# FFN weight split in two halves, and the context sum and small columns moved from VectorE to GpSimd, in a fused attention block on one Trainium2 core

## The reference

```
xn = layernorm(x)                        # no gain, no bias
# branch 1: linear attention and a gated feed-forward net (FFN)
q, k, v = split(xn @ Wqkv + bqkv);  qp, kp = elu(q) + 1, elu(k) + 1
attn = (qp @ (kp.T @ v)) / (qp @ sum(kp) + 1e-6)
x1 = layernorm(xn + attn) * g1 + b1
s = layernorm(x1 + (silu(x1 @ Wg + bg) * (x1 @ Wu + bu)) @ Wd + bd) * g2 + b2
# branch 2: three cycles that couple blocks of the features
gf = global_net(mean(xn over positions))          # 3 small layers, one value per batch
out = xn
repeat 3 times:
    tf = coupling_net(out)                        # 4 layers, one value per position
    out = out + (0.1 + range * (0.7*gf + 0.3*tf - 0.5) * 2) * twist(out)
result = x + s * silu(out)
```

## Time and profile before

| | |
|---|---|
| median of three runs | 165.39 us (165.28 to 165.51) |
| profiled execution, its own time | 163.89 us |
| its span in the trace | 162.1 us |
| PE busy, share of the span | 152.6 us, 94% |
| DVE busy | 137.4 us, 85% |
| ACT busy | 131.6 us, 81% |
| POOL busy | 116.9 us, 72% |
| mean granted PE clock | 0.986 of full |

### The profile page before, as it was taken

The page is one execution under the profiler, slowest core; times in us unless marked ns, Lnnn a source line. Parts: engine busy times, 40 slices in busy tenths (PEclk is TensorE's granted clock), DMA queues, the critical chain, the costliest instruction groups (busy, mean ns, idle before and its releaser), DMA issues.

```text
span 162.1 us, 3409 instructions
## 1 busy us (share of the span) xinstructions
PE 152.6 (94%) x934; PEld 117.0 (72%) x934; DVE 137.4 (85%) x549; ACT 131.6 (81%) x345; POOL 116.9 (72%) x202
## 2 busy tenths in 40 slices
PE   7889999999999899999999999999999999999940
PEld 7567988888888595545554565788888888888840
DVE  2998699899988998299999968978767999978893
ACT  3989796998999978999999986995648985844950
POOL 0078676699981869995089597379999998896573
PEclk9999999999999999999999999999999999999995
DMA  5997333030230000000000000000000110110113
GB/s 172 256 382 167 65 67 69 0 69 19 50 65 0 2 6 0 0 0 4 0 0 0 4 4 0 0 0 4 0 0 7 60 65 6 65 67 0 65 65 129
DMA packets 11923, 7.83 MB, mean 48 GB/s; under 512 B 8961, under 2 KB 9729, under 8 KB 11905
## 3 DMA queue, kind: packets, MB, share of 16 engines
q1 hardware_dynamic: 11472, 7.28, 15.5%
q10 hardware_dynamic: 432, 0.34, 0.6%
HBM read 3.43 MB, written 2.10 MB: 34 GB/s over the span
## 4 chain that ended last, share of the span: by engine, by line
PE 82%; ACT 7%; issue 3%; DMA 2%; DVE 2%; POOL 2%; POOLq 0%; ACTq 0%; DVEq 0%
PE bank L1074 11%; PE bank L1266 10%; PE bank L1191 7%; PE bank L1255 7%; PE bank L1257 7%; PE bank L1256 7%; PE bank L1203 4%; PE bank L1145 4%; PE bank L1216 4%; PE bank L1132 3%; PE bank L1133 3%; PE bank L1136 3%; PE bank L1156 3%; DMA col<-in_cols 2%; PE bank L1281 2%
## 5 line engine op out<-in xcount | busy, mean ns | idle before, releaser
L515 ACT ACTIVATE pq<-bank,bffn 128x512 f32<-128x512 f32 (+1 forms) x24 | 16.1, 682 | 9.3 <-PE bank L1257 9.3
L271 POOL TENSOR_TENSOR rstd<-ve,minus_half 128x4 f32<-128x4 f32 x21 | 21.2, 1011 | 1.7
L816 DVE SCALAR_TENSOR_TENSOR pq<-bank,bffn,pq 128x512 f32<-128x512 f32 (+1 forms) x24 | 17.6, 739 | 5.2 <-issue 2.4
L1255 PE MATMUL bank<-x_hi,ffn_hi 128*128 128x512 f32 (+1 forms) x48 | 20.5, 427 | 0.0
L1256 PE MATMUL bank<-x_lo,ffn_hi 128*128 128x512 f32 (+1 forms) x48 | 18.9, 395 | 0.0
L1257 PE MATMUL bank<-x_hi,ffn_lo 128*128 128x512 f32 (+1 forms) x48 | 18.9, 394 | 0.0
L1266 PEld LDWEIGHTS bank<-wd,pq 128*128 128x128 f32 x144 | 17.9, 191 | 1.3
L1266 PE MATMUL bank<-wd,pq 128*128 128x128 f32 x144 | 18.0, 274 | 0.0
L455 ACT ACTIVATE q_stage<-bank,col 128x512 f32<-128x512 f32 x24 | 16.0, 677 | 0.1
L269 POOL TENSOR_SCALAR nm<-mv 128x4 f32<-128x4 f32 x21 | 4.7, 223 | 15.4 <-DVE mv L653 15.4
L323 POOL TENSOR_TENSOR ab<-cpl 128x8 f32<-128x8 f32 x4 | 9.7, 2426 | 8.1 <-ACT cpl L487 8.0
(11 more groups left out here) (174 smaller groups left out, 457.7 us busy)
## 6 DMA issues: line engine op xcount, KB each, us to landing
x_tok<-in_x SPq DMA_DIRECT2D x8, 256.0 KB, 6.8
tx_tok<-xn_tok SPq DMA_DIRECT2D x16, 128.0 KB, 2.4
out<-pq SPq DMA_DIRECT2D x6, 256.0 KB, 2.0
r_tok<-in_w_ffn SPq DMA_DIRECT2D x1, 341.0 KB, 6.8
r_tok<-in_w_first SPq DMA_DIRECT2D x1, 320.0 KB, 3.5
out<-pq SPq DMA_DIRECT2D x2, 128.0 KB, 1.7
out<-pq ACTq DMA_DIRECT2D x1, 256.0 KB, 2.2
row<-in_rows SPq DMA_DIRECT2D x1, 192.0 KB, 6.3
```

Of the source, the lines that this page charges most:

```text
L271: return pool.tensor_tensor(rstd[i][:, b], ve[i][:, b], minus_half[:], ALU.pow)
L816: dve.scalar_tensor_tensor(out=hid[b % 2][0:m, c], in0=up_of(n)[0:m], scalar=bffn[0:m, CHUNKS + c:CHUNKS + c + 1], in1=sg[n % 2][0:m], op0 ...
L1255: pe.matmul(dst[0:m], ffn_hi[:, w], x1_hi[:, b], start=True, stop=False)
```

## The change

Four edits. ACT's split of the FFN weights becomes two instructions of 341 columns: the first behind tile 3 of batch 0, as the whole one was, the second behind tile 2 of batch 1. DVE's `ffn_lo` becomes two instructions too, behind `feature_k(6)` and at the end of batch 1's pass. `small_columns` goes from DVE to the head of POOL's pass 7 (`bias_rows`, once called in it, stays on DVE at its place). `ctx_sum` goes from DVE to the end of POOL's pass 7, as two instructions with a link between them, since POOL adds the offset and the two sums in separate steps.

```diff
+FFN_AFTER = ((0, 3), (1, 2))
...
+            def join_sums():
+
+                pool.wait_ge(sums_ready, 1)
+                pool.wait_ge(xT_hi_ready, BATCHES - 1)
+                pool.wait_ge(xT_lo_ready, BATCHES)
+                link(pool.tensor_scalar(ctx_sum[:], sum_hi, -OFFSET * SEQ, 0.0, ALU.add, ALU.add))
+                pool.tensor_tensor(ctx_sum[:], ctx_sum[:], sum_lo, ALU.add).then_inc(ctx_ready, 1)
+
+            def small_columns():
+
+                pool.wait_ge(cols_loaded, 16)
+                pool.tensor_scalar(half_b4[:], col[:, COL["cn_b4"]:COL["cn_b4"] + 1], 0.5, 0.0, ALU.mult, ALU.add)
...
             for b in range(BATCHES + 2):
                 if b + 2 < BATCHES:
                     norm_x(b + 2)
+                if b == BATCHES - 1:
+                    small_columns()
                 if b >= 2:
                     rstd_of(1, b - 2)
...
                 for done in {6: (0, 1, 2), 7: (3, 4, 5), 8: (6,), 9: (7,)}.get(b, ()):
                     negate_twisted(done)
+                if b == BATCHES - 1:
+                    join_sums()
...
+            def split_ffn(k):
+
+                act.wait_ge(ffn_loaded, 16)
+                act.wait_ge(cols_loaded, 16)
+                act.mul(ffn_hi[:, k * HID:(k + 1) * HID], ffn_raw[:, k * HID:(k + 1) * HID],
+                        col[:, COL["g1"]:COL["g1"] + 1]).then_inc(ffn_hi_ready, 1)
...
+                    if (b, t) in FFN_AFTER:
+                        split_ffn(FFN_AFTER.index((b, t)))
...
+            def ffn_low(k):
+
+                ks = slice(k * HID, (k + 1) * HID)
+                dve.wait_ge(ffn_hi_ready, k + 1)
+                dve.scalar_tensor_tensor(out=ffn_lo[:, ks], in0=ffn_raw[:, ks], scalar=col[:, COL["g1"]:COL["g1"] + 1],
+                                         in1=ffn_hi[:, ks].bitcast(F32), op0=ALU.mult,
+                                         op1=ALU.subtract).then_inc(ffn_ready, 1)
...
-                if b == BATCHES - 1:
-                    dve.wait_ge(sums_ready, 1)
-                    dve.wait_ge(xT_lo_ready, BATCHES)
-                    dve.scalar_tensor_tensor(out=ctx_sum[:], in0=sum_hi, scalar=-OFFSET * SEQ, in1=sum_lo,
-                                             op0=ALU.add, op1=ALU.add).then_inc(ctx_ready, 1)
...
                 feature_k(TILES * b + 1)
                 if b == 0:
-                    small_columns()
+                    bias_rows()
...
                 feature_k(TILES * b + 2)
+                if b == 1:
+                    ffn_low(0)
...
-            pe.wait_ge(ffn_ready, 1)
+            pe.wait_ge(ffn_ready, 2)
```

More of the change, by code:

```diff
@@ L293, in add_rows_to @@
                 return pool.tensor_tensor(yb[b % 2][:, ts], yb[b % 2][:, ts], x_tok[:, b, ts], ALU.add)
+            def join_sums():
[7 more added lines that the diff above has]
+                pool.tensor_scalar(half_b4[:], col[:, COL["cn_b4"]:COL["cn_b4"] + 1], 0.5, 0.0, ALU.mult, ALU.add)
+                pool.tensor_scalar(half_gb3[:], col[:, COL["gc_b3"]:COL["gc_b3"] + 1], 0.5, 0.0, ALU.mult, ALU.add)
+                pool.tensor_scalar(gain[:, 0:1], col[:, COL["range"]:COL["range"] + 1], W_GLOBAL, 0.0, ALU.mult, ALU.add)
+                pool.tensor_scalar(gain[:, 1:2], col[:, COL["range"]:COL["range"] + 1], W_TOKEN, 0.0,
+                                   ALU.mult, ALU.add).then_inc(cols_ready, 1)
             def norm_x1(b):
@@ L997, in _ @@
                 if b == 1:
[L998 to L1001, removed]
+                    ffn_low(1)
             add_eps(BATCHES - 2)
```

## The result

The changed kernel takes 171.31 us (median of four runs, 171.11 to 171.76) against 165.33 for the kernel before beside it: a ratio of 1.0363, with a 95% interval of 1.0341 to 1.0386. The prediction was +6.5 us and 171.9. The profiled execution took 171.11 us with a span of 169.3 us, 7.2 us more than the 162.1 of before; the medians differ by 6.0 us. The two numbers are not in conflict. Over all sessions the kernel before had medians of 165.33, 164.82, 164.65 and 164.42 us. Where time and span of an execution are both on record, the time was 1.8 to 3.1 us longer than the span, while the spans had medians of 162.1 to 162.3 us (23 executions in each of the three later sessions, 161.8 to 163.7).

A forecast was written before the change was run, and what follows sets the result against it. PE was taken to bound the kernel, busy for 152.6 of 162.1 us. A wait of 5.1 and a slow clock of 1.4 made +6.5 us on 165.39, so 171.9 us; range 170.2 to 173.5.

The forecast's parts named there:

- (b): Context sum behind POOL's pass 7: PE's matmul on it starts at 63.8 in place of 58.73, +5.1 us.
- faster: Rival: POOL's context sum comes in time for PE at 58.3 to 58.7; -0.6 us at most, 164.8 us; chance 0.02.
- (c): PE's clock falls while PE waits for the sum, then half pace for 3.2 us behind the wait: +1.4 us.
- a longer slow stretch: Rival: PE runs at half pace for 6.4 us behind the wait; +8.1 us, 173.5 us; chance 0.17.
- the first rival: PE waits for the sum, but its clock does not fall or is back at once: +5.1, 170.5 us; chance 0.16.
- the wait without the clock: Rival: only PE's wait for the sum is paid, no slow clock: +5.1, 170.5 us; chance 0.16.
- (a): Context sum leaves DVE: k-v copy starts 0.91 us earlier, PE's 0.6 us idle time goes; counted as nothing here.
- (d): Small columns leave DVE, four of 0.14 us at 12.45: they give nothing, 0.6 us at most without cover.
- (e): FFN split in halves on ACT and DVE in the early batches: 0, and 0.3 us at most either way.

The follow-up runs named there:

- the shorter waits: The changed kernel with POOL's sum earlier in pass 7, behind scale_x1 (first) or behind norm_x1 (second): 170.29 us and 168.82 us.

## Why the prediction was right

By its own steps:

(b), the wait, was forecast at +5.1 us with the matmul at 63.8. It started at 63.64, +4.9. Pass 7 began at 56.93 in place of 57.2, as POOL was free at 55.99 rather than 56.16 and the four small columns took 0.94 us rather than 1.04; the rest followed the rows: from its start to the sum's end 6.56 us, forecast 6.5. The chain that ended last lies on POOL for 8% of the span in place of 2%, some 10 us more, as foreseen. The sum moved alone gives all of the loss, and the sum at the head of the pass gives none of it. The rival "faster" had named its deciding point (the sum ready by 58.7), and at that point the loss did vanish. Its price of up to 0.6 us was too high: 0.27 us reached layer 2, and in that run other work took it back. That only 0.27 of 0.6 came through fits ACT, whose work on tiles 30 and 31 had no break there; this was read from the trace, not tested.

(c), the clock, was the mis-sized term: +1.4 us forecast, 2.3 measured, shown by the run that kept PE at work. I took the slow stretch from the start of the kernel, 3.2 us; here PE worked for 6.0 us at a granted 0.50. The forecast treated the length of the slow stretch as the same everywhere. The traces show 3.4, 5.2, 6.0 and 6.0 us of it in kernels that differ in little else. The second size was off as well, the other way: half of 6.0 us less 0.2 would be 2.8 us, and 2.3 were lost. The Trainium skill (TensorE: Matmul & The Clock Gate, Part 1) calls the number of slow products at a kernel's start run-variable, for one and the same kernel. The runs here show the stretch behind a wait, not that start, and it too differs between executions of one kernel (above, under the shorter waits).

So the length of the stretch was near that of the rival "a longer slow stretch" (6.4 us), not that of the forecast, and its cost lies between the forecast's 1.4 and the rival's 3.0. The time alone would hardly have told: 171.31 us lies 0.8 over the first rival's 170.5 and 0.6 under the forecast. It is the trace and the run with PE kept at work that rule out the wait without the clock.

Against the spans the two errors, -0.2 and +0.9, leave the forecast 0.7 us short (6.5 against 7.2). Against the medians it is 0.5 us too high (6.5 against 6.0). That it came so near there is in part luck: the carry assumed that the profiled execution stands to its median before as it does after. Before it was 1.5 us under its median, after it is 0.2 us under, and that difference of some 1.2 us turned 0.7 us too few into 0.5 us too many.

(a) was right in itself: DVE's copy started at 54.03 and PE did not wait for it, worth nothing here. (d) and (e) were right: 0, confirmed by the run with only these edits. In the changed kernel's ACT and DVE timelines the second half of the split sits at its new place, and ACT still idles before its next PE product:

```profile
18.40 0.61 ACT L451 ACTIVATE ffn_hi<-r_tok,col 128x341 fp32r<-128x341 f32 x1
18.89 0.38 ACT L441 ACTIVATE ek<-bank,minus_one 128x128 f32<-128x128 f32 x1
...
20.46 0.69 ACT L435 ACTIVATE q_stage<-bank,minus_one 128x512 f32<-128x512 f32 x1 [0.76 <-PE bank L1141]
...
18.77 0.70 DVE L939 SCALAR_TENSOR_TENSOR ffn_lo<-r_tok,col,ffn_hi 128x341 fp32r<-128x341 f32 x1
```

The exponential of tile 7 came 0.2 us later than in the earlier trace rows, within the 0.2 to 0.5 foreseen, and ACT's idle time before 20.46 shrank from 1.02 to 0.76.

The prediction held that no later idle time of PE could shrink, "since there are none", and in the changed kernel that was so but for the 0.2 us that it had counted. What it did not consider is that new idle time could arise: in the run with the early sum PE waits for 1.45 us, 45 us behind the place that was made faster.

What stays open: what sets the length of the slow stretch in one execution, what lets POOL in sooner or later beside DVE, and why the kernel before's time is now 1.8 and now 3.1 us longer than its span.

## What to carry to other kernels

When a small operation moves to an idle engine, read the whole stretch of that engine's queue in front of it, not the engine's share: POOL was free for 28% of the span, and the sum still came 5 us late, because it stood behind a pass that starts late. Put the price of PE's idle time on top of the wait; here the clock added half as much again, and a cheap test is to fill the wait with products nobody needs. And a gain at a busy place may come back as a loss elsewhere: before crediting one, look for engines that share something with the one that got faster.

## What was not expected of the hardware

- A POOL instruction with two SBUF inputs (128x8) stood for 12.96 us beside DVE's two-input instructions, 6.97 and 6.59 us in other runs, where one DVE instruction of that kind takes 0.34 us. DVE's next instruction overlaps the end of the one before in the trace. A wait of 0.40 us on DVE let POOL in at once, and the 12.96 us ended as DVE came to an instruction with one input in PSUM. But in the kernel before POOL got in at about 88.1 us, while DVE's two-input instructions went on without a break (every 0.26 us), so what decides is open. The Trainium skill (SBUF — State Buffer, "Who interferes with whom") has the loser blocked for the whole of an instruction; here it stayed blocked over up to some 48 of them.
- The granted clock fell 4.4 us behind PE's last product in the changed kernel, 3.6 us in the one with the sum alone moved, 4.05 and 2.0 us in the two with shorter waits, and 1.8 us at the end of the kernel before. A wait of 2.8 us was enough to pay for it in full.
- At half pace PE's loss is less than half of the stretch: 6.0 us of work at a granted 0.50 cost 2.3 us, which fits ACT's 1.28 us table load and gelus, which run beside PE's first work there at their old length (read from the timeline, not tested).
